# Expert sums laid out by token in two alternating PSUM banks, Silu through one bank, the last attention unit one slice earlier

## The reference

```python
x = x + attn0(layernorm(x)) + ffn0(layernorm(x))          # first layer, not touched
xn = layernorm(x)

def attn1(query):                     # query [T=8, B=512, 128]: 16 heads of 8, attends over the 8 sequences
    q, v = query @ Wq.T + bias_q, query @ Wv.T + bias_v   # Wq, Wv from a low-rank correction
    k = query @ k_w.T + k_b
    attn = softmax(einsum('nqd,nkd->nqk', q, k) * scale)
    out = einsum('nqk,nkd->nqd', attn, v)
    return out @ out_w.T + out_b

def ffn1(x):                          # 16 experts of 64 hidden units, 4 chosen per token, and a shared one of 128
    combine = grouped_top4_weights(x)                     # [tokens, 16]
    g = silu(einsum('th,efh->tef', x, w1_e)); u = einsum('th,efh->tef', x, w3_e)
    routed = einsum('tef,ehf,te->th', g * u, w2_e, combine)
    return routed + (silu(x @ w1_s.T) * (x @ w3_s.T)) @ w2_s.T

return x + attn1(xn) + ffn1(xn)
```

## Time and profile before

| | |
|---|---|
| time, median of 3 runs | 365.11 us (364.57 to 365.88) |
| the profiled execution | 366.06 us; its span, first to last instruction, 364.2 us |
| busy in the span | PE 307.7 us, DVE 311.2, POOL 239.0, ACT 186.4 |
| mean granted TensorE clock | 0.975 of full speed |

### The profile page before, as it was taken

How to read it: one execution, slowest core, us unless ns; L and a number is a source line. 1 busy time by engine, 2 the same in 40 slices (tenths; PEclk the granted TensorE clock), 3 DMA queues, 4 the chain that set the end, 5 groups by cost and what they waited for, 6 DMA issues and landing times.

```text
span 364.2 us, 4906 instructions
## 1 busy us (share of the span) xinstructions
PE 307.7 (84%) x1371; PEld 218.2 (60%) x1371; DVE 311.2 (85%) x825; ACT 186.4 (51%) x507; POOL 239.0 (66%) x152
## 2 busy tenths in 40 slices
PE   0569876989899887685988999999989999998993
PEld 0336664768677776563655755656657566565662
DVE  5995899987977868947989899898998989989792
ACT  3345756878678578491342632536236361352611
POOL 3185587655736531107779868889888998889651
PEclk9987999999999999699899999999999999999999
DMA  4690000000000000019633324225343252335000
GB/s 138 175 276 1 2 0 1 3 1 0 3 0 3 0 0 3 0 33 169 161 92 80 114 62 121 81 67 137 116 100 99 76 137 73 101 106 132 3 29 29
DMA packets 21311, 24.81 MB, mean 68 GB/s; under 512 B 2428, under 2 KB 12068, under 8 KB 21284
## 3 DMA queue, kind: packets, MB, share of 16 engines
q1 hardware_dynamic: 20336, 24.09, 25.0%
q10 hardware_dynamic: 820, 0.39, 0.4%
q0 software_dynamic: 128, 0.01, 0.0%
HBM read 22.13 MB, written 2.36 MB: 67 GB/s over the span
## 4 chain that ended last, share of the span: by engine, by line
DVE 37%; PE 25%; issue 15%; POOL 12%; ACT 7%; DMA 3%; SPq 1%; ACTq 0%; DVEq 0%; POOLq 0%
PE Q L917 11%; POOL prod_qk L856 8%; PE VN L917 7%; PE T L917 3%; DVE att L1549 3%; DVE rope_b L1326 3%; DVE rope_a L1324 3%; DVE hid L1587 3%; DVE sgc L1574 3%; POOL prod_pv L866 2%; PE T L913 2%; DVE bst L1167 2%; DVE attn L1356 2%; ACT L750 1%; DMA cw<-comb_table 1%
## 5 line engine op out<-in xcount | busy, mean ns | idle before, releaser
L856 POOL TENSOR_TENSOR prod_qk<-qkv 128x1024 f32<-128x1024 f32 x32 | 76.3, 2395 | 17.0 <-DVE above L1419 15.2
L866 POOL TENSOR_TENSOR prod_pv<-prob,qkv 128x1024 f32<-128x1024 f32 x32 | 69.6, 2195 | 18.5 <-DVE att L1549 17.0
L917 PE MATMUL VN<-hid,w 128*128 128x512 f32 x144 | 74.6, 599 | 1.5 <-DVE hid L1587 1.5
L917 PE MATMUL Q<-xT_hi,w_hi 128*128 128x512 f32 x72 | 52.1, 724 | 0.2 <-ACT sg L750 0.2
L1587 DVE TENSOR_TENSOR hid<-T,sgc 128x512 f32<-128x512 f32 x64 | 43.4, 679 | 0.0
L1535 DVE TENSOR_REDUCE scr<-prod_qk 128x128 f32<-128x1024 f32 x32 | 38.8, 1213 | 5.0 <-POOL prod_qk L856 4.9
L917 PE MATMUL Q<-bias,ones 128*128 128x400 f32 (+1 forms) x64 | 30.3, 474 | 15.1 <-ACT v_ext L638 7.1
L917 PE MATMUL T<-xT_hi,w_hi 128*128 128x512 f32 x72 | 30.8, 428 | 9.4 <-DVE hid L1587 9.3
L1549 DVE TENSOR_REDUCE att<-prod_pv 128x128 f32<-128x1024 f32 x32 | 38.3, 1197 | 0.0
L750 ACT ACTIVATE VN<-Q 128x512 f32<-128x512 f32 x32 | 18.6, 582 | 36.7 <-PE Q L917 29.1
L750 ACT ACTIVATE ND<-Q 128x512 f32<-128x512 f32 x32 | 18.6, 582 | 35.7 <-PE Q L917 24.7
(11 more groups left out here) (176 smaller groups left out, 747.9 us busy)
## 6 DMA issues: line engine op xcount, KB each, us to landing
cw<-comb_table SPq DMA_DIRECT2D x64, 256.0 KB, 4.5
out_x<-fin SPq DMA_DIRECT2D x8, 256.0 KB, 4.5
x<-in_x SPq DMA_DIRECT2D x2, 256.0 KB, 3.0
wraw<-in_w1T SPq DMA_DIRECT2D x1, 512.0 KB, 4.1
w3raw<-in_w3T SPq DMA_DIRECT2D x1, 512.0 KB, 4.7
w<-in_w2T SPq DMA_DIRECT2D x1, 512.0 KB, 5.7
rope_s<-in_c_sin ACTq DMA_DIRECT2D x1, 256.0 KB, 4.9
rope_c<-in_c_cos SPq DMA_DIRECT2D x1, 256.0 KB, 5.4
```

The lines of the kernel that those rows point to most:

```text
L856: pool.tensor_tensor(prod_qk[:, t % 2], bc(qkv2[:, TH * half + t, j, 0:D], 1, NB), qkv2[:, :, j, D:2 * D], ALU.mult).then_inc(qk_prod, 1)
L866: pool.tensor_tensor(prod_pv[:, t % 2].rearrange("p (h e) b -> p b h e", e=HD), bc(prob[:, t].rearrange("p h b -> p b h"), 3, HD), qkv2[:, ...
L917: return pe.matmul(o, lhsT, rhs, start=start, stop=stop)
```

## The change

The `down` product swaps its operands: `hid` is now loaded as weights, in four tiles of 128 tokens, and `w2` streams, so that the sum comes out with tokens in the partitions. It goes to VK and Q2 by turns of the slot (`YB`), and the attention's projection (`attention_product`) is added on top in the same bank. `yT_evac`, the tile `yT` and the four transposes of `output_back` are gone. The bias can no longer ride on ACT's copy: `bout2` is loaded as a full 128x128 tile and POOL adds it to `x` (`biased`), once per unit, ahead of `less_max`. Silu has one bank, ND0 (`SB`), and from slice 2 of a slot on it waits for `sgc` of the slice before; ND1 takes the attention's transposes. The last unit starts at slice 64, its maximum in the same slice as its last scores; its projection comes at p = 9, and its residual at p = 10 in two halves, each with a store of its own.

```diff
-        SB = (ND0, ND1)
+        SB = ND0
+        YB = (VK, Q2)
-        BASE = (5, 14, 23, 31, 40, 48, 57, 65)
-        LAST = BASE[NSLOT - 1] + 15
+        BASE = (5, 14, 23, 31, 40, 48, 57, 64)
+        LAST = BASE[NSLOT - 1] + 12
+        END = NSLOT - 1
...
             def gate(n, s):
                 act.wait_ge(g_ps, NS * n + s + 1)
-                if s >= 3:
-                    act.wait_ge(sgc_ready, (NS - 1) * n + s - 2)
+                if s >= 2:
+                    act.wait_ge(sgc_ready, (NS - 1) * n + s - 1)
                 else:
                     after(act, hid_ready, NS * n + s - 1)
-                gated = SB[side(n, s)] if s > 0 else sg
+                gated = SB if s > 0 else sg
...
-                act.activation(yT[:, (n - 1) % 2], tiles(VK), ACT.Identity, bias=bout2[:, 0:1]).then_inc(yT_ready, 1)
...
+            def biased(n):
+                j, half = place(n)
+                b = slice(TH * half, TH * half + TH)
+                if n == 0:
+                    pool.wait_ge(ld_w2, 64)
+                pool.tensor_tensor(x[:, b, j, :], x[:, b, j, :], bc(bout2[:, :], 1, TH), ALU.add)\
+                    .then_inc(x_biased, 1)
...
                 next_qk(0)
+                biased(n)
                 less_max(n)
...
                 pe.wait_ge(hid_ready, NS * n + s + 1)
                 if s == 0:
-                    after(pe, yT_ready, n)
-                mm(VK[:, :], w2[:, routed_slice(s) % NS, :], hid[:, s % 3, :], s == 0, s == NS - 1).then_inc(y_ps, 1)
+                    after(pe, fin_ready, n - 1)
+                    if n == 1:
+                        pe.wait_ge(r_step, R_MASKED)
+                for t in range(TH):
+                    o = slice(t * P, (t + 1) * P)
+                    m = mm(YB[n % 2][:, o], hid[:, s % 3, o], w2[:, routed_slice(s) % NS, :], s == 0 and t == 0, False)
+                m.then_inc(y_ps, 1)
...
-            def output_back(n):
-                pe.wait_ge(yT_ready, n + 1)
+            def attention_product(n):
                 pe.wait_ge(attT_ready, n + 1)
                 for t in range(TH):
-                    pe.matmul(Q2[:, t * P:(t + 1) * P], yT[:, n % 2, t, :], ident[:, :], is_transpose=True, start=True,
-                              stop=False)
-                    m = mm(Q2[:, t * P:(t + 1) * P], attT[:, t, :], wout2[:, :], False, True)
+                    o = slice(t * P, (t + 1) * P)
+                    m = mm(YB[n % 2][:, o], attT[:, t, :], wout2[:, :], False, t == TH - 1)
                 m.then_inc(yback_ps, 1)
...
-                    if p == 11:
-                        output_back(u)
+                    if p == (9 if u == END else 11):
+                        attention_product(u)
...
+                dve.wait_ge(x_biased, n + 1)
                 dve.wait_ge(fin_free, n + 1)
-                V.tensor_tensor(fin[:, n % 2], x[:, TH * half:TH * half + TH, j, :], tiles(Q2), ALU.add)\
-                    .then_inc(fin_ready, 1)
+                parts = 2 if n == END else 1
+                for h in range(parts):
+                    a, b = TH // parts * h, TH // parts * (h + 1)
+                    V.tensor_tensor(fin[:, n % 2, a:b], x[:, TH * half + a:TH * half + b, j, :],
+                                    tiles(YB[n % 2])[:, a:b], ALU.add).then_inc(fin_ready, 1)
...
-                first = (-4, -3, -2, -1) if u == 0 else (-8, -7, -2, -1)
+                first = (-4, -3, -2, -1) if u == 0 else (-7, -6, -1, 0) if u == END else (-8, -7, -2, -1)
...
-                if p == 13:
+                if p == (10 if u == END else 13):
                     residual(u)
```

More of the change, by code:

```diff
@@ L115, in build @@
         wout2 = sb("wout2", [P, D])
-        bout2 = sb("bout2", [P, 1])
+        bout2 = sb("bout2", [P, D])
         rope_c = sba("rope_c", [P, NJ, 2, D])
@@ L306, in build @@
         attT = sb("attT", [P, TH, P])
-        yT = sb("yT", [P, 2, TH, P])
         fin = sb("fin", [P, 2, TH, D])
@@ L326, in build @@
         y_ps = sem("y_ps")
-        yT_ready = sem("yT_ready")
+        x_biased = sem("x_biased")
         qk_prod = sem("qk_prod")
@@ L414, in comb_bank @@
         def comb_bank(h):
-            return (T0, Q2)[h]
+            return (T0, ND1)[h]
         def side(n, s):
@@ L478, in _ @@
             sp.dma_start(wout2[:, :], d["wout2T"]).then_inc(ld_w2, 16)
-            sp.dma_start(bout2[:, :], d["bout2"].rearrange("(p a) -> p a", a=1)).then_inc(ld_w2, 16)
+            sp.dma_start(bout2[:, :], d["bout2"].partition_broadcast(P)).then_inc(ld_w2, 16)
             sp.sem_inc(fin_free, 2)
@@ L532, in _ @@
                 slot(n)
-            for n in range(NSLOT - 2, NSLOT):
-                store(n)
-                stored_of(n)
+            store(END - 1)
+            j, half = place(END)
+            for h in range(2):
+                sp.wait_ge(fin_ready, END + 1 + h)
+                settle(sp)
+                ts = slice(TH // 2 * h, TH // 2 * (h + 1))
+                sp.dma_start(ov[:, TH * half + TH // 2 * h:TH * half + TH // 2 * (h + 1), j, :], fin[:, END % 2, ts])\
+                    .then_inc(stored, 16)
+            sp.wait_ge(stored, 16 * (NSLOT + 1))
         def exp_of(act):
@@ L743, in gate @@
                 act.wait_ge(g_ps, NS * n + s + 1)
-                if s >= 3:
-                    act.wait_ge(sgc_ready, (NS - 1) * n + s - 2)
+                if s >= 2:
+                    act.wait_ge(sgc_ready, (NS - 1) * n + s - 1)
                 else:
                     after(act, hid_ready, NS * n + s - 1)
-                gated = SB[side(n, s)] if s > 0 else sg
+                gated = SB if s > 0 else sg
                 act.activation(gated[:, :], QB[side(n, s)][:, :], ACT.Silu).then_inc(sg_ready, 1)
             def attT_evac(u):
[L753 to L760, removed]
-                act.activation(yT[:, (n - 1) % 2], tiles(VK), ACT.Identity, bias=bout2[:, 0:1]).then_inc(yT_ready, 1)
+                evac(attT[:, :, :], tiles(ND1), (attT_ps, u + 1), [(yback_ps, u)], attT_ready)
             act.wait_ge(ld_w2, 64)
@@ L774, in _ @@
                     combT_evac(1)
-                if s == 1 and n <= NSLOT:
-                    yT_evac(n)
         @block.gpsimd
@@ L1100, in attention_transposes @@
                 pe.wait_ge(att_ready, n + 1)
-                after(pe, fin_ready, n)
-                transposes(Q2, lambda t: att[:, t, :], signal=attT_ps)
-            def output_back(n):
-                pe.wait_ge(yT_ready, n + 1)
+                after(pe, attT_ready, n)
+                transposes(ND1, lambda t: att[:, t, :], signal=attT_ps)
+            def attention_product(n):
                 pe.wait_ge(attT_ready, n + 1)
                 for t in range(TH):
-                    pe.matmul(Q2[:, t * P:(t + 1) * P], yT[:, n % 2, t, :], ident[:, :], is_transpose=True, start=True,
-                              stop=False)
-                    m = mm(Q2[:, t * P:(t + 1) * P], attT[:, t, :], wout2[:, :], False, True)
+                    o = slice(t * P, (t + 1) * P)
+                    m = mm(YB[n % 2][:, o], attT[:, t, :], wout2[:, :], False, t == TH - 1)
                 m.then_inc(yback_ps, 1)
@@ L1142, in _ @@
                 for u, p in units(k):
-                    if p == 11:
-                        output_back(u)
+                    if p == (9 if u == END else 11):
+                        attention_product(u)
                     if p == 8:
-                        if u == 0:
-                            pe.wait_ge(r_step, R_MASKED)
                         if u == 2:
@@ L1151, in _ @@
                 if k == COMB_AT:
-                    pe.wait_ge(fin_ready, 2)
+                    pe.wait_ge(attT_ready, 2)
                     comb_transposes(1)
@@ L1573, in weighted @@
                         dve.wait_ge(ld_cw[r // 2], 32 * (n + 1))
-                    V.tensor_tensor(sgc[:, k, :], SB[k][:, :], cw[:, r // 2, r % 2, :], ALU.mult)\
+                    V.tensor_tensor(sgc[:, k, :], SB[:, :], cw[:, r // 2, r % 2, :], ALU.mult)\
                         .then_inc(sgc_ready, 1)
```

## The result

The changed kernel takes 367.21 us (median of 16 runs) where the kernel before takes 365.79 (16 runs beside them): ratio 1.0039, 95% interval 1.0024 to 1.0054. One of its sixteen runs took 399.82 us at a mean granted clock of 0.752, against 0.97 to 0.99 in the others, and the ratio leaves it out. A second series gave 1.0033 (1.0016 to 1.0049). By the two ratios it is slower by 1.2 to 1.4 us; forecast were +0.7, and a range of 363.1 to 368.3 that holds the result.

The account below looks back on a forecast made before the run. PE, DVE and POOL were all near full, with DVE idle mostly at the exponentials, where ACT and POOL arrive together. Terms 0.1 + 2.4 + 0.55 - 2.44 + 0.05 = +0.7 on 365.11 gave 365.8 us; range 363.1 to 368.3.

Parts of the forecast that it names:

- POOL's addition: Bias addition ahead of `less_max`: 1.15 us late at each of units 3 and 5, 0.07 at 4 and 6; +2.4 us.
- The end: From the last `hid` to `fin`: 2.03 us instead of 4.47, with only 16 loads and products left there; -2.44 us.
- The last unit: Last unit started a slice ahead: DVE has one more `sgc` and `hid` behind its exponential, last `hid` later by +0.55 us.
- Behind the start of the last `fin`: Two halves of `fin`, each with its own store, end some 0.05 us later than one; +0.05 us.
- The swapped `down`: Eight narrow products a slice hold PE 0.03 us longer, counted only on few slices just ahead of an exponential; +0.1 us.
- The transposes and ACT's copy: PE gains 0.43 us a slot, but nobody waits for it in slots 0 to 6; counted as nothing, slot 7 with the end.
- Silu's single bank: Silu's wait for the previous slice's `sgc` just fits ahead of the exponential of unit 5; counted as nothing.
- within 0.3%: The case that the measured time can't be told from no change, some 1.1 us either way; chance 0.42.
- the side that had 0.34: The case that the changed kernel is slower by over 0.3%; chance 0.34.
- (a): Rival: POOL's addition costs nothing at units 3 and 5, as POOL gets there earlier; 362.9 to 363.5 us; chance 0.24.
- (b): Rival: Silu's single bank delays the exponentials, 0.5 us at each of 8 units, +4.7 in all, 369.8 us; chance 0.27.
- (c): Rival: weight loads pace the narrow products of `down`, 1.2 us more a slice, some 80 us, 445 us; chance 0.03.

Follow-up runs that it names:

- e1: Changed kernel with POOL's addition of the bias moved from ahead of `less_max` to between the second and third product with v; 0.9952 and 0.9966 of the kernel before.
- e8: Kernel before, with only the output bias added to `x` by POOL ahead of `less_max` instead of in ACT's copy; 1.0090 of the kernel before.
- e6: Changed kernel with POOL's addition made twice per unit, the first time into a spare tile; 1.0247 of the kernel before.
- e5: Kernel before, with only Silu's single PSUM bank and its wait for `sgc` of the slice before; 1.0005 of the kernel before.
- e4: Changed kernel with every other Silu going to a second tile, in SBUF, with the old waits; 397.57 us, 1.0858 of the kernel before.

## Why the prediction was right, and where it was off

**The mechanism was right.** The first profile after splits the +1.20 by the starts of `fin`: +1.26 up to the third (unit 3), +0.22 to the fourth, +1.23 to the fifth (unit 5), +0.16 to the sixth, +0.65 to the last `hid`, -2.25 from there to the last `fin`, -0.07 after it.

- *POOL's addition*, +2.4 by the sum, is 2.87 by the first four of these, less the 0.17 that e1 has in the same stretch, so 2.7; e8 has 2.76. Right in place at units 3 and 5, too small by 0.3. Two steps of it were off. "I take 1.20, less 0.05 of overlap 1.15" came from half a product; the spacing is 1.23 to 1.24, near the addition to `x` of 1.27 in the earlier trace rows, the same operation with the same output. And at units 4 and 6 "0.07 each sticks out" took the wrong path. There `less_max` ends 0.97 and 0.96 us ahead of the end of the table load in the changed kernel, so the exponential is not late. What grew is the wait of `scores` for the product behind `less_max`, from 1.23 to 1.35 at unit 4 and from 1.21 to 1.36 at unit 6; the 0.35 ahead of `sgc` at unit 4, 0.24 before, e1 has as well (0.34). e6 makes this second door plain. The groups of the kernel before show it too. "DVE's idle stretches lie mostly at the exponentials" holds for 5.1 + 2.8 us of them, and 4.9 lie ahead of `scores`:

```profile
L1574 DVE TENSOR_TENSOR sgc<-ND,cw 128x512 f32<-128x512 f32 x32 | 21.8, 682 | 6.9 <-ACT ND L750 5.1 <-DMA cw<-comb_table 1.8
L1574 DVE TENSOR_TENSOR sgc<-VN,cw 128x512 f32<-128x512 f32 x32 | 21.8, 681 | 2.8 <-ACT VN L750 2.8
...
L1535 DVE TENSOR_REDUCE scr<-prod_qk 128x128 f32<-128x1024 f32 x32 | 38.8, 1213 | 5.0 <-POOL prod_qk L856 4.9
```

- *The end*, -2.44, is -2.25. "15 x 0.111 + 0.27" left out that the first load has nothing to pass behind: it starts at 361.06, and the last product ends at 362.06 + 1.12 = 363.18, 2.12 us where I had 1.94. Of the 0.18, 0.11 is that load; the other 0.07 is the last eight, 1.12 us instead of 1.05.
- *The last unit*, +0.55, is +0.65. *Behind the start of the last `fin`*, forecast +0.05, it is -0.07.
- *The swapped `down`*, 0.1: from the first `fin` to the sixth e1 takes 114.65 us and the kernel before 114.48. That +0.17 holds all of the change except POOL's place and the end.
- *The transposes and ACT's copy*, nothing before slot 7: right, since e1, where POOL's term is gone, shows no gain ahead of the end.
- *Silu's single bank*, nothing: shown by e5.

The forecast's sum without POOL's term is 0.1 + 0.55 - 2.44 + 0.05 = -1.7; e1, which is just that, measures -1.5 and -1.4. The undersized addition is 0.3 of the 0.5 between +0.7 and +1.2, and the end most of the rest. They moved the times past the forecast's "within 0.3%": 0.39% and 0.33% lie just over it, on the side that had 0.34, while both intervals, 0.24 to 0.54% and 0.16 to 0.49%, contain 0.3%. The 367.21 us also lie 0.2 above the forecast's own range, 364.7 to 367.0; only the part added for the rivals holds them. That is the baseline more than the change: the forecast stood on a median of three runs, 365.11, and sixteen gave 365.79.

**The rivals.** (a) is refuted by the waits of 2.35 and 2.30 us where it needed 1.06; what it claimed becomes true only when the addition is moved (e1). (b) is refuted by e5. (c) is refuted by `down` in 1.05 us. In these rows a load costs time only where no product runs ahead of it: the one at 361.06 holds its product up until 361.17. These 0.11 us agree with the 107 ns that 128 columns give by the formula of the Trainium skill ("TensorE: Matmul & The Clock Gate", section "LDWEIGHTS (loading the stationary operand)").

## What to carry to other kernels

Before putting work on an engine with idle time, ask where in its list the idle time lies: the same addition of 1.29 us a unit cost 2.7 us a run just ahead of the instruction that ACT, and DVE behind it, waits for, and nothing between two products where POOL waits for DVE anyway. Follow both things behind the insertion, the next instruction and the one after it, to whoever waits for each. And when a span's change is small, compare from a marker behind the stretch whose clock varies.

## What the runs showed of the hardware that was not expected

In e4 half of DVE's `sgc` multiply two SBUF tiles instead of one in PSUM and one in SBUF. The two groups:

```profile
L1582 DVE TENSOR_TENSOR sgc<-sg,cw 128x512 f32<-128x512 f32 x32 | 57.6, 1800 | 5.1 <-ACT sg L758 3.1 <-DMA cw<-comb_table 2.0
...
L1582 DVE TENSOR_TENSOR sgc<-VN,cw 128x512 f32<-128x512 f32 x32 | 21.7, 678 | 4.8 <-ACT VN L758 4.8
```

The same product takes 1.80 us on average instead of 0.68: 32 x 1.12 = 36 us, more than the 30 us that e4 lost against the changed kernel. Single ones show why. DVE's and POOL's timelines at one of them:

```profile
276.38 2.37 DVE L1582 TENSOR_TENSOR sgc<-sg,cw 128x512 f32<-128x512 f32 x1
```

```profile
276.05 2.16 POOL L863 TENSOR_TENSOR prod_pv<-prob,qkv 128x1024 f32<-128x1024 f32 x1 [2.62 <-DVE att L1557]
```

POOL's product started first and ended at 278.21; DVE's ended 0.54 us later, at 278.75. All 32 run so: each starts while a POOL instruction runs and ends 0.48 to 0.58 us after one has ended, and the shortest, 0.69 us, is the one that started when POOL had 0.11 us to go. The Trainium skill ("SBUF — State Buffer", section "Who interferes with whom") says that a DVE instruction with two SBUF inputs contends with a GpSimd instruction that reads SBUF, and that issue order decides which of the two blocks; this trace agrees. In the changed kernel, with POOL busy 68% of the span, it is a reason for Silu to stay in PSUM.
